# A first pass over the image with four rows on a partition: tap products in quarters of the array, and the downsampled rows' frequencies made in the same pass

## The reference

```
# block 1: on pairs of channels
d    = conv(x, w_down, stride 2, pad 1, groups 256)     # 3x3 taps, 2 channels -> 1: (8, 256, 64, 64)
label = kmeans(scaled d[0], 8 clusters, 10 iterations)  # on the 256 channels of image 0
v5   = mean of d over the channels of a cluster         # (8, 8, 64, 64)
mu, var = two-part Gaussian mixture of v5, 10 EM iterations
gate = sigmoid(...)[label]
y    = bilinear_x2(repeat(gate*d + d, 2) * w_up) + x
# block 2: attention over channels, on 8x8 low cosine frequencies
P    = 8x8 lowest cosine frequencies of 128x128
q, k = Wq, Wk on y projected on P;  v = Wv y;  out = gamma * attention + y (+ bias)
```

## Time and profile before

| | |
|---|---|
| median of three runs | 2971.88 us |
| profiled execution | 2971.82 us, span 2970.0 us |
| PE busy | 2610.5 us, 88% of the span |
| DVE, ACT, POOL busy | 2000.4, 1261.3, 1040.5 us |
| first pass | to about 971 us |
| gather pass | 971 to 1264 us |
| mixture pass | 1264 to 1440 us |
| second pass | 1440 us to the end |

### The profile page before, as it was taken

How to read it: one execution, slowest core, us unless ns; L and a number is a source line. 1 busy time by engine, 2 the same in 40 slices (tenths; PEclk the granted TensorE clock), 3 DMA queues, 4 the chain that set the end, 5 groups by cost and what they waited for, 6 DMA issues and landing times.

```text
span 2970.0 us, 47824 instructions
## 1 busy us (share of the span) xinstructions
PE 2610.5 (88%) x18374; PEld 1710.4 (58%) x18374; DVE 2000.4 (67%) x2285; ACT 1261.3 (42%) x3336; POOL 1040.5 (35%) x772
## 2 busy tenths in 40 slices
PE   8999999999998799768499988988888888888886
PEld 2222222333332465334289888877778877788776
DVE  3666666565555322065489998988788888888886
ACT  0000000000000423223377777766666676666764
POOL 5444444444442000000044444443333443343443
PEclk9999999999999899879799999999999999999999
DMA  9999999999998826500489999999999999999999
GB/s 345 322 319 324 316 322 320 308 326 318 324 317 248 241 107 238 188 1 0 176 314 416 416 414 413 398 372 369 359 379 364 382 372 384 364 385 380 385 399 336
DMA packets 605236, 940.07 MB, mean 317 GB/s; under 512 B 189922, under 2 KB 452450, under 8 KB 601443
## 3 DMA queue, kind: packets, MB, share of 16 engines
q1 hardware_dynamic: 605026, 937.21, 88.7%
HBM read 632.01 MB, written 303.04 MB: 315 GB/s over the span
## 4 chain that ended last, share of the span: by engine, by line
DMA 35%; PE 8%; DVE 3%; ACT 2%; issue 1%; SPq 1%; POOL 0%; DVEq 0%; ACTq 0%
DMA out<-second_x 27%; PE second_o L1302 6%; DMA second_dd<-downsampled 4%; DMA second_x<-in_x 3%; DVE second_x L1526 1%; DVE second_left L1075 1%; PE second_mid_t L1272 1%; SPq L1108 1%; ACT second_mid L1391 1%; PE second_st L1162 1%; DVE second_mid L1507 1%; ACT second_left L1403 0%; POOL second_left L1075 0%; ACT second_part L1391 0%; PE second_zt_t L1285 0%
## 5 line engine op out<-in xcount | busy, mean ns | idle before, releaser
L1302 PE MATMUL second_o<-second_right,second_left 128*128 128x128 f32 x8192 | 1084.4, 282 | 110.2 <-issue 45.2
L1075 POOL TENSOR_TENSOR second_left<-second_mid_copy,second_coef_rep 64x1024 f32<-64x1024 f32 x256 | 608.2, 2376 | 1419.9 <-ACT second_mid_copy L1412 1390.2
L1302 PEld LDWEIGHTS second_o<-second_right,second_left 128*128 128x128 f32 x8192 | 1002.6, 196 | 143.9 <-issue 132.8
L1526 DVE SCALAR_TENSOR_TENSOR second_x<-second_o,second_shift,second_x 128x512 f32<-128x512 f32 x1024 | 736.3, 739 | 225.3 <-PE second_o L1302 116.8
L241 PE MATMUL first_conv<-first_x,first_band 128*64 128x512 f32 (+1 forms) x3072 | 717.4, 616 | 13.5 <-POOL first_band L200 10.6
L210 DVE TENSOR_TENSOR first_product<-first_freq,first_cols 128x4096 f32<-128x4096 f32 x64 | 283.2, 4425 | 395.7 <-PE first_freq L257 395.7
L241 PEld LDWEIGHTS first_conv<-first_x,first_band 128*64 128x64 f32 x3072 | 225.6, 135 | 499.0 <-issue 468.3
L193 POOL TENSOR_TENSOR first_band<-first_shift,first_w_all 128x576 f32<-128x576 f32 x256 | 289.9, 1154 | 493.3 <-PE first_conv L241 486.7
L223 ACT ACTIVATE first_staged<-first_conv 128x512 f32<-128x512 f32 x128 | 76.5, 597 | 873.6 <-DMA downsampled<-first_staged 648.8
L1391 ACT ACTIVATE second_mid<-second_dd,all_inter 128x128 f32<-128x128 f32 x1024 | 313.3, 388 | 83.5 <-DMA second_dd<-downsampled 81.2
L1391 ACT ACTIVATE second_part<-second_dd,all_inter 128x128 f32<-128x128 f32 x1024 | 313.3, 388 | 3.2
(11 more groups left out here) (224 smaller groups left out, 1559.6 us busy)
## 6 DMA issues: line engine op xcount, KB each, us to landing
first_x<-in_x SPq DMA_DIRECT2D x256, 1024.0 KB, 10.4
second_x<-in_x SPq DMA_DIRECT2D x256, 1024.0 KB, 14.3
out<-second_x SPq DMA_DIRECT2D x256, 1024.0 KB, 16.4
gather_d<-downsampled SPq DMA_DIRECT2D x24, 2048.0 KB, 12.8
downsampled<-first_staged SPq DMA_DIRECT2D x128, 256.0 KB, 8.2
second_dd<-downsampled SPq DMA_DIRECT2D x64, 512.0 KB, 15.0
second_p<-in_p_cols SPq DMA_DIRECT2D x1, 4096.0 KB
gates_ft<-gather_rows SPq DMA_DIRECT2D x64, 32.0 KB, 2.0
```

The source lines that it names most:

```text
L1075: return eng.tensor_tensor(left[a][rows, odd:HALF:2, :, :].rearrange("p n (t s) g -> p n t s g", t=T), turned[rows, :, :, :].unsqueeze(3). ...
L1302: last = nc.tensor.matmul(ob[n][:, r, :], left[a][:, r, n, :], right[a][:, r, :], start=True, stop=True)
L1526: nc.vector.scalar_tensor_tensor(out=xt[i][:, n // S, n % S, rows, :], in0=ob[n][:, :, :], scalar=shift[:, n:n + 1], in1=xt[i][:, n // S, ...
```

## The change

In the first pass a partition holds four rows of a channel instead of two. A tile is half of a group: two units, each on 64 partitions (32 blocks of four rows, two channels), loaded by two transfers of 64 partitions with contiguous runs of 2 KB. There are 7 tile buffers of twice the size. A tap product works on 64 rows of the array (one unit) and 64 or 32 columns: rows 1 and 3 of a block reach both output rows of it (64 columns), rows 0 and 2 one (32 columns). Two units stand in the row halves, each with a PSUM bank of its own, and two tiles in the column halves. The bands have six 32-column masks, made by one POOL instruction for a tile. A downsampled row pair leaves in four transfers of 32 partitions; 12 staging buffers instead of 4 keep the copies until PE has multiplied them by row cosines (`project_low`, every fourth group), and DVE makes the column sums of these with the same kind of instruction pair as for `x`. The result goes to a new tensor `projected_low`.

The gather pass loses the frequency work and its list of steps: PE transposes, makes the Gram matrix in parts, runs the rounds and then the means, and nothing else. It has five image buffers instead of four; small tiles live in `wv` and `xps`, which are not loaded yet. The list `later`, with 16 more transfers for `xpu` from `projected_low`, is loaded by SP in the mixture pass, and DVE waits for it before it uses `xpu`.

```diff
-SLOTS1 = 14
-WEIGHTS1 = 8
+BLOCK1 = 4
+BLOCKS1 = H // BLOCK1
+TILES1 = GROUPS1 * 2
+SLOTS1 = 7
+WEIGHTS1 = 4
+EDGES = [(1, (2, 0)), (3, (0, 2)), (0, (1,)), (2, (1,))]
+BANDS = [dh for _r, dhs in EDGES for dh in dhs]
-STAGED = 4
+STAGED = 12
+SPAN = 4
...
-    xv = x.rearrange("b (c s) (i r) w -> c (s i) b (r w)", s=S, r=2)
+    xv = x.rearrange("b (c s) (i r) w -> c (s i) b (r w)", s=S, r=BLOCK1)
+    xdv = xd.rearrange("b t g (i e w) -> (t g) e i b w", e=2, w=WD)
...
+                def load(tile):
+                    g, a, slot = tile // 2, tile % 2, tile % SLOTS1
+                    if tile >= SLOTS1:
+                        sp.wait_ge(freq_made, (tile - SLOTS1) // 2 + 1)
+                    for k in range(2):
+                        sp.dma_start(xt[slot][k * 64:k * 64 + 64, :, :, :].rearrange("p b r w -> p b (r w)"),
+                                     xv[g * GROUP1 + 2 * k + a]).then_inc(x_in[slot], 16)
...
+                    for a in range(2):
+                        for e in range(2):
+                            at = a * 64 + e * 32
+                            sp.dma_start(xdv[2 * pair + a, e], staged[pair % STAGED][at:at + 32, :, :]
+                                         ).then_inc(stored[pair % STAGED], 16)
...
+                sp.wait_ge(low_summed, GROUPS1 // SPAN)
+                sp.dma_start(xpd, low_freq[:, :, :, :].rearrange("p n b v -> p n (b v)")).then_inc(low_out, 16)
...
+                for g in range(GROUPS1):
+                    if g > SPAN and g % SPAN == 1:
+                        dve.wait_ge(low_summed, g // SPAN)
+                    sum_cols(g)
+                    if g >= SPAN and g % SPAN == 0:
+                        sum_low_cols(g // SPAN - 1)
+                sum_low_cols(GROUPS1 // SPAN - 1)
...
+                    def product(r, n, width, place, dw, first, last):
                         left = 1 if dw < 0 else 0
                         at = dw + 2 * left
+                        for a in range(2):
+                            for k in range(2):
+                                tile, part = 2 * g + a, slice(k * 64, k * 64 + 64)
+                                made = nc.tensor.matmul(
+                                    conv_ps[(2 * g + k) % CONV_BANKS][a * HD + place:a * HD + place + width * BLOCKS1,
+                                                                      :, left:],
+                                    band[tile % WEIGHTS1][part, dw + 1, n:n + width, :].rearrange("p n i -> p (n i)"),
+                                    xt[tile % SLOTS1][part, :, r, at:at + 2 * (WD - left) - 1:2],
+                                    start=first, stop=last)
+                        return made
+                    for dw in (0, 1, -1):
+                        product(1, 0, 2, 0, dw, dw == 0, False)
+                        product(3, 2, 2, 0, dw, False, False)
+                    for dw in (0, 1, -1):
+                        product(0, 4, 1, 0, dw, False, dw < 0)
+                        made = product(2, 5, 1, BLOCKS1, dw, False, dw < 0)
+                    made.then_inc(conv_made, 1)
...
+                def project_low(n):
+                    pe.wait_ge(conv_copied, 2 * SPAN * (n + 1))
+                    if n > 0:
+                        pe.wait_ge(low_taken, n)
+                    for j in range(2):
+                        for q in range(4):
+                            pair = 2 * SPAN * n + 2 * q + j
+                            last = nc.tensor.matmul(low_ps[32 * q:32 * q + 32, :, :], low_rows[:, j, :],
+                                                    staged[pair % STAGED][:, :, :], start=j == 0, stop=j == 1)
+                    last.then_inc(low_made, 1)
                 for g in range(GROUPS1):
-                    convolve(2 * g)
-                    convolve(2 * g + 1)
+                    convolve(g)
+                    if g >= SPAN and g % SPAN == 0:
+                        project_low(g // SPAN - 1)
                     project(g)
...
+RING = 5
+RING_OF = [0, 1, 4, 2, 3, 0, 1, 4]
+X_BANKS = 4
...
+                for n in range(GROUPS):
+                    turn_x(0, n)
+                for n in range(GROUPS):
+                    pe.wait_ge(x_copied, n + 1)
+                    add_gram(0, 0, n, 1)
+                for n in range(GROUPS + 2):
+                    if n < GROUPS:
+                        turn_x(1, n)
+                    if n >= 2:
+                        pe.wait_ge(x_copied, GROUPS + n - 1)
+                        side = add_gram(0, 1, n - 2, 1)
+                        last = add_gram(1, 0, n - 2, T)
...
+                for dst, src in later:
+                    sp.dma_start(dst, src).then_inc(later_in, 16)
+                sp.wait_ge(later_in, len(later) * 16)
```

More of the change, by code:

```diff
@@ L1 @@
+import itertools
 import concourse.bass as bass
@@ L185, in _ @@
             @block.gpsimd
             def _(pool):
[L187 to L200, removed]
+                pool.wait_ge(const_in, 64)
@@ L235, in convolve @@
                         left = 1 if dw < 0 else 0
                         at = dw + 2 * left
[L237 to L244, removed]
@@ L277, with gather_pass @@
 WIDE = P // K
[L280 removed]
+def gather_pass(nc, cst, consts, xd, ohn, oh_t, ft, work, pieces):
     with Scope(nc, "gather") as sc:
         ring = [sc.sb(f"d{i}", [P, T * POS]) for i in range(RING)]
[L285 to L292, removed]
[L293 to L302 removed]
@@ new lines, in gather_pass @@
+        rows_sb = [work[:, i, :] for i in range(2)]
+        gram, square = work[:, 2, :].rearrange("p (t g) -> p t g", t=T), work[:, 3, :]
+        rep = pieces[:, 0:2, :, :].rearrange("p a s k -> p (a s k)").rearrange("p (t a k) -> p t a k", t=T, k=K)
+        placed = pieces[:, 2, :, 0:6 * K]
+        hi, lo, den, inv, x2, low, best = (pieces[:, 3, 0, T * n:T * n + T] for n in range(7))
+        x2_parts = pieces[:, 3, 1, 0:T * GROUPS].rearrange("p (t n) -> p t n", t=T)
+        wt, prod, dist, near, score, oh = (pieces[:, 4 + n, 0, 0:T * K].rearrange("p (t k) -> p t k", t=T)
+                                           for n in range(6))
@@ L500, in _ @@
+                for t in range(T):
+                    act.wait_ge(rep_t, t + 1)
+                    nc.scalar.activation(oh_t[:, t, :], bank_x[t][:, 1, :], ACT.Copy).then_inc(rep_copied, 1)
             @block.tensor
             def _(pe):
-                pe.wait_ge(const_in, 32)
+                pe.wait_ge(const_in, 16)
                 def turn_x(t, n):
@@ L580, in multiply @@
-                def multiply(k):
-                    b, u, slot = k // UNITS_F, k % UNITS_F, k % SLOTS
-                    if u == 0 and b >= 2:
-                        pe.wait_ge(freq_read, b - 1)
-                    pe.wait_ge(copied[slot], k // SLOTS + 1)
-                    for n in range(2):
-                        last = nc.tensor.matmul(freq_ps[b % 2][n * UV:(n + 1) * UV, 0:T * P], q_sb[:, 2 * u + n, :],
-                                                dT[slot][:, n, :], start=u == 0, stop=u == UNITS_F - 1)
-                    last.then_inc(multiplied[slot], 1)
@@ new lines, in _ @@
+                for n in range(GROUPS):
+                    pe.wait_ge(x_copied, n + 1)
[7 more added lines that the diff above has]
+                        last = add_gram(1, 0, n - 2, T)
+                side.then_inc(gram_made, 1)
```

442 lines of the change are left out of this document (179 added, 263 removed).

## The result

The changed kernel takes 3409.24 us (median of 4 runs, 3401.64 to 3412.21), the kernel before 2973.34 us beside it: a ratio of 1.1464 with a 95% interval of 1.1441 to 1.1487. Slower, as forecast, but by 436 us and not 283, and above the upper end of the range (3320). The profiled execution has a span of 3409.6 us.

What follows compares the result with a forecast made beforehand. PE bounds the first pass, DMA a close second; afterwards DMA, at 20.5 us a group. 2971.82 + 376 (first pass) + 5 (tail) + 0 (mixture) - 98 (gather) = 3255 us; range 2740 to 3320.

Steps and rivals of the forecast that it cites:

- The bound before, the bound after, and PE's part: First pass: PE bounds it before, DMA after; PE needs 12.4 us a group, tap products 8.3 of it.
- the signs: First pass: tap products wait some 8 us a group, loads at 200 to 255 GB/s, PE busy six tenths.
- Rival 3: First pass: row halves don't run side by side, PE takes 20.6 us a group, 3257 us in all; chance 0.04.
- The loads: First pass: 64-partition loads run at 230 GB/s, so 4.19 MB take 18.2 us a group.
- Rival 2: First pass: loads half way at about 300 GB/s, 16.3 us a group, 2986 us in all; chance 0.05.
- The stores: First pass: 2.3 us a group for the 2048 pieces; SP's 12 issues, 6.2 us, lie below either pace.
- Rival 1: First pass: loads keep the wide rate, 400 GB/s, 12.8 us a group, 2762 us in all; chance 0.34.
- Gather pass: Gather pass as a whole: -98 us, between -70 and -115, from first round, rounds and means.
- First round: Gather pass: clustering starts 61 us into the scope instead of 104.9, -44 us.
- rounds: Gather pass clustering: +13 us on 68.9 (between -3 and +28), as PE's clock may drop; wrong above 8.8 us each.
- The means: End of the gather pass: 52 us instead of 119.2, -67 us.
- Mixture pass: Mixture pass: about 52 us of moved loads hide beside 176 us, cost 0; wrong if VectorE waits near its end.

Runs made afterwards that it cites:

- e1_wide: Changed kernel with the two units of a tile made neighbours, so each load is one transfer over 128 partitions; 2990.98 us.
- e4: Changed kernel with each load into 64 partitions issued as two into 32; 3399.87 us.
- e9: Changed kernel, loads still narrow, with the stores of the downsampled image issued from ACT's queue instead of SP's; 3213.06 us.
- e5: e1_wide with the stores of the downsampled image issued from ACT's queue instead of SP's; 2757.53 us, ratio 0.9302 to the kernel before.
- e8: e5 with the means' row stores on ACT's queue and five unread PE products added to each clustering round; 2746.88 us, ratio 0.9274.
- e3: Changed kernel with a tile's two loads writing the even, then the odd partitions instead of lower and upper half; 2906.08 us.

## Why the prediction was wrong

- *The bound before, the bound after, and PE's part.* Right, and the signs came: waits of 8.3 us a group for 8, PE at six tenths, 210 GB/s. Row halves of the array run side by side: 96 products in 8.53 us at full clock in e1_wide (511.53 us; forecast 8.3), a group of 12.47 us once nothing holds PE (forecast 12.4). Rival 3 falls.
- *The loads.* The step that failed is a term of the sum: "I take 230, nearest to the share of partitions". Narrow loads by themselves run at 215 GB/s: 19.5 us a group for 18.2, some 83 us of the 130 in 64 groups. The mechanism (half of the paths) held, and the share itself, 220, was nearer than the 230 taken; but as a rule, a share by partitions covered does not hold: by it 32 partitions had to be half as fast as 64, and they are as fast (e4). Rival 2 falls too: where loads run alone the rate is 215 and not 300.
- *The stores.* The second term that was too small. The sum adds 2.3 us for their pieces and takes their issue as free ("6.2 us, below either pace"). On SP's queue between narrow loads they cost 2.9 us a group (e9), and SP takes some 19 us to issue the eight of a group, not eight times 0.52. The 0.6 us more are some 40 us of the 130.
- The estimate by the Trainium skill's page "SBUF — State Buffer" that stood beside the sum, 22.5 us and 3383 us, came within 0.2% and 0.8%. In part that is luck: that estimate rests on 208 GB/s (196 and 6%), below the 215 measured, and on 2.3 us of stores, below the 2.9.
- *Rival 1* gave 2762 us to wide loads. With the wide rate alone the kernel takes 2991; its first pass at 16.25 us a group loses more than the gather pass gives back. 2762 is reached only when the queue is mended as well (e5: 2757.5), and then by offsets: the first pass comes out 17 us below the rival's, the gather pass 23 above, and the second pass, which the change leaves as it is, 9 below.
- *Gather pass.* First round and rounds right (59.2 us for 61; 7.3 us a round, under 8.8). Some 10 of the +11 us of the rounds are the granted clock (e8). The means failed by 25 us. The last load lands some 46 us into the stage, not 38, since each copy waits for the row stores of two images before, and these for their issue and for the loads beside them; and some 30 us of row stores follow it, for the 14 that the forecast had.
- *Mixture pass.* Right: 175.5 us with the loads beside it, and VectorE waits for none near its end.
- *The range* ended at 3320. Its likeliest case went no lower than 220 GB/s for the loads, and had no room for dearer stores and for means 25 us longer at the same time.

## What to carry to other kernels

A transfer that writes one half of the partitions moved at about half the rate here, with pieces of 1 KB and of 2 KB (79 ns for 46, 162 for 84); pair neighbours so that every load covers both halves, before counting what a new layout saves on the compute engines. Then read a queue as an order, not as a sum of bytes: here eight small stores ahead of large loads on one queue left the engines half empty, until the loads were mixed between them, in halves, or the stores went to another engine's queue. A DMA share near 1.0 does not say that nothing can be gained: it read 1.02 in a window with half-empty stretches, and moving the stores away gave 13% of a group.

## What the runs showed that was not expected

- Even partitions in one transfer and odd ones in the next reach 322 GB/s; the lower and then the upper half 211. Size and number of the pieces and transfers of a group are the same. With 14.8 us a group, e3 is even faster than e1_wide (16.25), whose loads come in one transfer each; why was not tried.
- Stores beside narrow loads, on a second queue, raise the total from 211 to 243 GB/s. The loads by themselves are no faster (214 GB/s for 215), though a 2 KB piece takes 139 ns for 159: the length of a piece is no measure of the rate when pieces of one engine overlap (share 1.09).
- Once PE no longer waits, its clock follows: 0.81 granted in the first pass of the kernel after, 1.00 with wide loads and a mended queue, and 96 products take 8.5 us instead of the 9.9 and 10.5 of the two groups shown.
